# Sixteen rows of a gather fetched by SyncE with addresses from registers, and GpSimd's gather cut to 112 partitions

## What is computed

```python
msg = relu(x[src] + edge_attr)                       # layer 0
h = 2 * x + segment_sum(msg, dst)
f = gelu(bn(h) @ W1.T + b1) @ W2.T + b2
x = layernorm(x + bn(h + f))
h = gelu((x[src] + edge_attr) @ W1m + b1m)           # layer 1
agg = segment_sum(h @ W2m + b2m, dst) / max(degree, 1)
u = gelu(agg @ W1u + b1u) @ W2u + b2u
out = layernorm(x + layernorm(x + u) * gamma + beta) # in outline
```

## Time and profile before

| | |
|---|---|
| three runs | 2637.56, 2638.18, 2649.71 us; median 2638.18 us |
| the profiled execution | span 2139.9 us from its first to its last instruction; its own time on the device is not given beside it |
| granted TensorE clock, mean | 0.975 |
| instructions | 38235 |
| POOL | busy 1593.0 us, 74% |
| PE, DVE, ACT | busy 87%, 71%, 60% |
| DMA | 569.42 MB, mean 266 GB/s |

### The profile page before, as it was taken

One profiled execution on the slowest core, in us unless ns is written; L12 is line 12 of the kernel. 1 busy time (PEld: TensorE's weight loads), 2 busy tenths in 40 slices (PEclk: granted clock), 3 DMA queues, 4 the chain that ended last, 5 costly groups with the idle time before them and its releaser, 6 DMA issues.

```text
span 2139.9 us, 38235 instructions
## 1 busy us (share of the span) xinstructions
PE 1853.7 (87%) x9034; PEld 1516.1 (71%) x9034; DVE 1515.9 (71%) x3743; ACT 1287.3 (60%) x2642; POOL 1593.0 (74%) x1695
## 2 busy tenths in 40 slices
PE   4998888888888888888879899899899899999997
PEld 3876767666666666666667777777777777777775
DVE  4676666666666666666666787877777887787786
ACT  5766566566566565565555565656665665665664
POOL 7777777777777777777577777777777777777774
PEclk9999999999999999999999999999999999999998
DMA  8999999999999999999788787777778777777783
GB/s 251 341 336 310 320 309 318 306 311 312 316 303 315 314 306 318 306 314 316 234 268 241 216 232 224 232 227 227 229 227 234 225 227 224 227 235 223 226 236 107
DMA packets 349112, 569.42 MB, mean 266 GB/s; under 512 B 48328, under 2 KB 214212, under 8 KB 349044
## 3 DMA queue, kind: packets, MB, share of 16 engines
q1 hardware_dynamic: 268858, 349.78, 51.3%
q0 software_dynamic: 79824, 218.08, 33.3%
q10 hardware_dynamic: 362, 0.85, 0.1%
HBM read 500.59 MB, written 67.94 MB: 266 GB/s over the span
## 4 chain that ended last, share of the span: by engine, by line
POOL 47%; issue 18%; PE 15%; DMA 13%; DVE 5%; DVEq 1%; ACT 1%; ACTq 0%; POOLq 0%
POOL m_all L678 46%; DMA m_all<-in_x,src_p 7%; DMA m_all<-y_scratch,src_u 5%; PE bank L1136 4%; PE bank L1202 3%; PE bank L1161 2%; PE bank L1244 1%; PE bank L1107 1%; DVE bank L1549 1%; DVEq L1482 1%; DVE m_all L1526 1%; PE bank L1044 1%; DMA win_i<-in_dst 1%; ACT m_all L854 1%; PE bank L1118 1%
## 5 line engine op out<-in xcount | busy, mean ns | idle before, releaser
L678 POOL DMA_INDIRECT m_all<-y_scratch,src_u x831 | 789.3, 950 | 256.0 <-issue 238.9
L678 POOL DMA_INDIRECT m_all<-in_x,src_p x816 | 777.3, 953 | 248.8 <-issue 233.7
L1136 PE MATMUL bank<-m_all,sel 128*128 128x257 f32 x1664 | 454.2, 396 | 141.2 <-ACT m_all L854 139.7
L1202 PE MATMUL bank<-w1m_sb,e_all 128*128 128x256 f32 x2040 | 514.2, 393 | 1.5 <-DVE m_all L1669 1.5
L854 ACT ACTIVATE m_all<-m_all 128x512 f32<-128x512 f32 x415 | 261.1, 629 | 379.3 <-DVE m_all L1526 378.3
L1136 PEld LDWEIGHTS bank<-m_all,sel 128*128 128x128 f32 x1664 | 299.7, 192 | 244.3 <-issue 126.6
L1526 DVE TENSOR_TENSOR m_all<-bank,m_all 128x512 f32<-128x512 f32 x415 | 285.1, 688 | 235.8 <-DMA m_all<-in_x,src_p 215.8
L906 ACT ACTIVATE m_hi<-bank 128x512 fp32r<-128x512 f32 x412 | 245.7, 596 | 295.2 <-DVE bank L1549 293.2
L1549 DVE TENSOR_TENSOR bank<-bank,m_all 128x512 f32<-128x512 f32 x415 | 288.9, 696 | 183.6 <-DMA m_all<-y_scratch,src_u 122.9
L1202 PEld LDWEIGHTS bank<-w1m_sb,e_all 128*128 128x128 f32 x2040 | 380.6, 197 | 45.2 <-DVE m_all L1669 2.0
L1244 PE MATMUL bank<-m_lo,sel 128*128 128x256 f32 x824 | 263.7, 344 | 86.3 <-DVE sel L1446 74.5
(11 more groups left out here) (196 smaller groups left out, 1948.5 us busy)
## 6 DMA issues: line engine op xcount, KB each, us to landing
e_all<-in_edge SPq DMA_DIRECT2D x416, 256.0 KB, 5.5
e_all<-in_edgeT SPq DMA_DIRECT2D x204, 256.0 KB, 3.7
ez<-in_edgeT SPq DMA_DIRECT2D x103, 384.0 KB, 5.0
z_scratch<-zc SPq DMA_DIRECT2D x103, 384.0 KB, 6.0
e_all<-z_scratch SPq DMA_DIRECT2D x103, 256.0 KB
m_all<-y_scratch,src_u POOLq DMA_INDIRECT x831, 3.7
e_all<-z_scratch SPq DMA_DIRECT2D x103, 128.0 KB
m_all<-in_x,src_p POOLq DMA_INDIRECT x816, 5.6
```

What stands on the lines that cost most here:

```text
L678: pool.indirect_dma_start(out=m_sb[n % ROUND][:, t, :], out_offset=None, in_=table, in_offset=bass.IndirectOffsetOnAxis(ap=sources(g, u), ...
L1136: return pe.matmul(psum[:, 0:D + 1], selection[:, u, :].bitcast(F32), m_all[:, slot, u % 2, 0:D + 1], start=(u == 0), stop=(u == TILES - 1 ...
L1202: last = pe.matmul(z_bank(s)[:, t * D:(t + 1) * D], eT_sb[s % ERING][:, k, t * P:(t + 1) * P], w1m_sb[:, k, :], start=(k == 0), stop=(k == ...
```

## The change

SP fetches the last 16 rows (partitions 112 to 127) of the last tile of every second group, g = 3, 5, ..., 101, in both passes, one row of 1 KB per transfer. The row's number comes from a new list `row_src`, read four numbers at a time into SP's registers. POOL's gather of these tiles names 112 partitions. DVE waits for SP's rows (`row_in`) beside POOL's gather. DVE also makes the list, with two small copies at the start. The sixteen rows of pair p = 4g + 3 = 8b + 15 are issued in four batches of four, at SP's steps 8b + 4, 8b + 6, 8b + 8 and 8b + 10.

```diff
+SHARED = 16
+AT_ONCE = 4
...
+        row_src = sb("row_src", [G, 2, SHARED], I32)
...
+        def shared(g):
+            return g % 2 == 1 and 2 <= g < G - 1
+
+        def rows_in(i, s):
+            q, j = divmod(s, PAIRS)
+            if j < 3 or q % 2 == 0 or known(i) and not shared(PER_ROUND * i + q):
+                return None
+            return 16 * SHARED * (i + q // 2)
...
+            def gather_rows(table, second, n):
+                b, r = divmod(n // 2 - 2, SHARED // AT_ONCE)
+                g = 2 * b + 3
+                if n % 2 or b < 0 or not shared(g):
+                    return
+                slot = (PAIRS * g + 3) % ROUND
+                if not r and second:
+                    if b == 0:
+                        sp.wait_ge(y_out, 16 * C)
+                        sp.wait_ge(xab_out, 32 * C)
+                        sp.wait_ge(a_clear, C)
+                    if PAIRS * g + 3 >= ROUND:
+                        sp.wait_ge(added, M + PAIRS * g + 3 - ROUND + 1)
+                elif not r:
+                    if b == 0:
+                        sp.wait_ge(row_src_made, 1)
+                    if PAIRS * g + 3 >= ROUND:
+                        sp.wait_ge(pair_summed, PAIRS * g + 3 - ROUND + 1)
+                numbers = nc.values_load_multi_w_load_instructions(
+                    row_src[g:g + 1, second, r * AT_ONCE:(r + 1) * AT_ONCE], engines=[sp.engine], min_val=0, max_val=N - 1,
+                    skip_runtime_bounds_check_because="they number nodes")[1]
+                for k, v in enumerate(numbers):
+                    p = P - SHARED + r * AT_ONCE + k
+                    sp.dma_start(m_all[p:p + 1, slot, 1, 0:D], table[bass.ds(v, 1), :]).then_inc(row_in[slot // TILES], 16)
...
             def edges_first(n, early=False):
...
+                gather_rows(x, 0, n)
 
             def edges_second(n, early=False):
...
+                gather_rows(y_dram, 1, n)
...
                 for t in range(first, 2):
                     u = 2 * j + t
+                    rows = P - SHARED if u == TILES - 1 and shared(g) else P
                     pool.indirect_dma_start(
-                        out=m_sb[n % ROUND][:, t, :], out_offset=None, in_=table,
-                        in_offset=bass.IndirectOffsetOnAxis(ap=sources(g, u), axis=0),
+                        out=m_sb[n % ROUND][0:rows, t, :], out_offset=None, in_=table,
+                        in_offset=bass.IndirectOffsetOnAxis(ap=sources(g, u)[0:rows, :], axis=0),
...
+                if i == 1:
+
+                    dve.tensor_copy(row_src[:, 0, :], ends_f[1].rearrange("g (p u) -> g p u", u=TILES)[:, P - SHARED:P, TILES - 1])
+                    dve.tensor_copy(row_src[:, 1, :], ends_f[1][:, GROUP - SHARED:GROUP]).then_inc(row_src_made, 1)
...
                 dve.wait_ge(m_in[s], m_used(i))
+                if rows_in(i, s) is not None:
+                    dve.wait_ge(row_in[s // TILES], rows_in(i, s))
...
                 dve.wait_ge(m_in[s], m_used_again(i) - 16 * tile_of(i, s) - (16 if s == ROUND - 1 else 0))
+                if rows_in(i, s) is not None:
+                    dve.wait_ge(row_in[s // TILES], rows_in(i, s) + rows_first_pass)
```

More of the change, by code:

```diff
@@ L360, in build @@
         ends_ready, lists_turned, lists_made = map(sem, ("ends_ready", "lists_turned", "lists_made"))
+        row_src_made, row_in = sem("row_src_made"), sems("row_in", 2)
         bn_made, acc_zero, w_fused, w_kept = map(sem, ("bn_made", "acc_zero", "w_fused", "w_kept"))
@@ L463, in e_used_again @@
             return each * (2 * i) + each * (s // ERING + 1) + 16 * (M // ERING)
+        def shared(g):
[5 more added lines that the diff above has]
+            return 16 * SHARED * (i + q // 2)
+        rows_first_pass = 16 * SHARED * (ROUNDS - 1)
+        assert not shared(1) and shared(3) and G % 4 == 0 and not shared(G - 1) and shared(G - 3)
         def last_pair(i, s):
```

## The result

The changed kernel takes 2892.1 us (median of four runs, 2888.7 to 2899.8) against 2638.5 us of the kernel before (2637.6 to 2649.7): ratio 1.0957 [1.0931, 1.0984], slower by 254 us. Predicted were 2633 us, in a range of 2622 to 2675.

A forecast was written before the change was run, and what follows sets the result against it. The prediction took POOL's full queue of gathers to bound both passes. Its only non-zero term, 5.9 us saved by shorter gathers, gave 2638.2 - 5.9 = 2632.3, rounded to 2633 us, range 2622 to 2675.

The forecast's parts named there:

- What bounds the kernel: POOL's full gather queue sets both passes, 1.25 us per gather, 20.0 us per two groups; 498.3 us outside the span carried over.
- What it adds to SP: SP's queue: 16 transfers and four reads per two groups, 7.2 + 1.6 us, making 14.5 of 20.0 us; costed at nothing.
- the forecast's 2 to 12 us saved: Whole kernel: shorter POOL gathers save 2 to 12 us, time 2626 to 2640 us; chance 0.41.
- rival 1: POOL's 112-row gather takes as long as one of 128; sum 0 to +1.1 us, 2639 us; chance 0.24.
- rival 3: SP becomes the bound from 0.79 us per row; at 1.0 us 330 us more, near 2960; chance 0.13.
- POOL's part: 100 gathers of 112 rows for 128, each 59 ns shorter (between 0 and 118), saving 5.9 us.
- The DMA engines: One-row transfers sit whole on one engine, raising its pass 1 share from 0.94 to 0.98 to 1.04; costed at nothing.
- rival 2: One DMA engine fills up in pass 1; at 130 ns per row +40 us, 2673 us; chance 0.17.
- Waits and late rows: SP's slot wait is met on arrival and rows land 5 us before DVE uses them; costed at nothing.
- rival 4: Rows land late for DVE, beyond 5 us of margin; costs only if it grows, then the same end as rival 2 or rival 3.
- DVE's instructions and the two small copies: DVE's 100 waits with arithmetic, nothing (uncovered 7 us); two copies at the start, nothing, at most 1.1 us.

The follow-up runs named there:

- e0_before: The kernel before, unchanged, run again to get a second trace at the slow pace: 2637.2 us, 0.9999 of before.
- z2: Changed kernel with fixed row numbers, register reads, moves and arithmetic replaced by plain counts on a spare semaphore, at the slow pace: 2821.7 us, 1.0708 of before.
- e1_gather112: Kernel before with POOL's part only: 98 gathers name 112 partitions, SP fetches nothing; slow pace: 2633.8 us, 0.9981 of before.
- e2: Changed kernel with its 1600 one-row transfers from fixed row numbers, no register reads or address arithmetic; slow pace: 2648.0 us, 1.0035 of before.
- e7: Kernel before plus, at 400 places on SP, a loop of four turns counting a spare semaphore, no row transfers; quick pace: 2149.9 us, 1.0006 of before.
- sessions 2 and 3: Two sets of runs, each made together on one chip, at the quick pace; the kernel before took 2149.0 and 2150.0 us.
- session 6: A set of runs made together on one chip, at the slow pace: the change and two of its part variants; the kernel before took 2635.6 us.
- e6: Changed kernel with one read of one number and one computed address per batch of four, other three rows fixed; quick pace: 2148.9 us, 1.0003 of before.

## Why the prediction was wrong

**What bounds the kernel.** This failed first. "The 498.3 us between them are outside every view; the edit puts nothing there that I can see, and I carry them over whole" took the second pace for work before and after the trace. e0_before shows the span to be 2640.6 us when the run is 2642. Everything built on the POOL clock (1.25 us per gather, 20.0 us for two groups, SP's 14.5 of 20.0) was true of the trace and not of the executions that were timed. At the slow pace the clock of pass 1 is 1196.0 / 816 x 16 = 23.5 us for two groups. POOL now waits for others, at the start of each group, the two waits below:

```profile
1005.05 0.95 POOL L678 DMA_INDIRECT m_all<-in_x,src_p  x1 [2.01 <-remote]
1006.30 0.95 POOL L678 DMA_INDIRECT m_all<-in_x,src_p  x1 [0.30 <-issue]
...
1016.75 0.95 POOL L678 DMA_INDIRECT m_all<-in_x,src_p  x1 [1.97 <-PE bank L1136]
```

**What it adds to SP.** The step that carries the loss: "It has room, narrowly at the dear end... I cost it at nothing". The sum of it was right at the quick pace: arithmetic 37 ns, move 29, transfer 253 (240 in pass 2), reads 495 ns, so 9.4 us for four batches where 8.8 were worked out, and nothing at the end (0.9992, an interval of -4 to 0 us, which can't tell the forecast's 2 to 12 us saved from rival 1's nothing). The room was smaller than forecast all the same: in pass 1 SP had 116 us of longer gaps left in 1028.6, 2.3 us of 20.0 where 5.5 were worked out. At the slow pace the four batches are 18.5 us. Less the four reads at their median of 0.5 us, a row costs (4.63 - 0.5) / 4 = 1.03 us. This is rival 3's place and mechanism: its threshold was 0.79 us per row, and at 1.0 it gave 330 us. With the true clock of 23.5 us in pass 1 the same line gives 18.5 + 5.7 - 23.5 = 0.7 us, only 35 us for its 50 times, and nothing in pass 2, whose clock is 25.1 us. The rest comes from what SP does besides: in pass 1 it has 308 us of other instructions and 141 us of gaps beside them, 449 us or 8.8 us per two groups for the 5.7 assumed, and 18.4 (940 us) + 8.8 = 27.2 of the 27.8 us that two groups take after. So SP's records account for the new length of pass 1. The other instructions did not grow as a sum (306 us in e0_before, at the same pace). The edge loads did, from 328 to 419 ns in the middle, but they read 418 ns at the quick pace too, so that is no mark of the slow one. What rival 3 had wrong was its reason: "none has an address from a register". The register address is 66 ns more (37 + 29), and plain counts in its place keep 76% of the loss (z2). What the loss follows is how many small instructions SP executes beside its transfers, and no term of the sum priced a pause per instruction.

**POOL's part.** Mis-sized: 59 ns were taken, and the 100 gathers of 112 rows read 932 ns in the middle against 949 for the others, 934 against 956 in the mean, at the quick pace and nearly the same at the slow one. The third of these rows, POOL at the quick pace, is the shared tile of group 49:

```profile
507.16 0.95 POOL L726 DMA_INDIRECT m_all<-in_x,src_p  x1 [0.30 <-issue]
508.41 0.95 POOL L726 DMA_INDIRECT m_all<-in_x,src_p  x1 [0.30 <-issue]
509.67 0.93 POOL L726 DMA_INDIRECT m_all<-in_x,src_p  x1 [0.30 <-issue]
```

That is 17 to 22 ns, 1.7 to 2.2 us for 100, nearer to rival 1's nothing than to the 5.9 us of the sum. e1_gather112 alone gave -4 us [-9, -1] at the slow pace, where POOL isn't the bound, of which the shorter gathers would explain some 2; the rest is open. What the Trainium skill says (DMA: Bandwidth & Descriptors, "Anatomy of one DMA — SWDGE (gpsimd) path"), that many descriptors can be emitted before their number costs noticeably, agrees with these rows.

**The DMA engines (rival 2).** Right, costed at nothing. A one-row transfer left two packets (272058 on SP's queue for 268858 before, 3200 for 1600 transfers), which fits data that go whole through one engine, as the prediction had read from ACT's packets. In pass 1 the share rose from 0.94 to 0.96 at 313 GB/s for 312 and the time stood still at the quick pace; at the slow pace e2 has all the transfers for 10 us, where the rival put 40.

**Waits and late rows (rival 4).** Right at the quick pace: DVE waited for the rows twice, 6.2 us in all. At the slow pace it waited 39 times and 233 us; the rows are late because SP is, so it is rival 3's end, as the prediction had it. DVE's instructions and the two small copies show no cost at the quick pace.

**What stays open.** What makes the slow pace. Single instructions of POOL and DVE last as long in both (the gathers 949 ns in the middle, DVE's adds of line 1605 or 1549 695 and 696 ns in the mean), while SP's instructions stall. PE's matmuls are a little longer (line 1136: 425 ns in the mean for 396), at a granted clock of 0.888 in e0_before for 0.975 in the trace of before. The clock alone isn't the reason: one run of e7 at the quick pace had a granted clock of 0.845 and took 2160.8 us. It isn't a matter of one chip: by their records sessions 2 and 3 (quick) and session 6 (slow) ran on the chip with the same number. Nor was it settled why counts alone cost 46 us in one session and 100 us in another.

One rival for the stalls was not tested: the recording of the execution itself. The traces of the slow pace have all instructions (43529 of the change in both), but few of the records of semaphores: 14492 in e0_before for 54487 in before, 17159 for 57453 for the change. So records were lost at the slow pace and hardly or not at the quick one, and no run was made with less recorded. What made one may have made the other, or the recording may hold up an engine whose instructions come dense. It also means that "another core or an unknown queue" and "remote" in the slow views are partly missing records, and that who released a wait there is less sure than at the quick pace.

## What to carry to other kernels

Set the span of the trace against the time of the runs before anything else: when they differ by more than a few us, the trace may be of another pace, and its bound may not be the bound that is timed. When work is moved to a queue that seems free, count its instructions and not only their durations, and price them also at a slower issue (0.3 to 0.4 us each here), above all where one instruction becomes many small ones. And compare parts within one session: the same kernel lay 46 us above before in one and 100 us in another.

## What the runs showed of the hardware

In these runs the same program took 2149 or 2638 us, with all kernels of a session at one pace. At the slow one SyncE stalled some 0.7 us again and again, more than once in five instructions in the change (1542 of 6803), and the stalls hit counts, register moves, branches and transfers alike. A loop of four turns did not help against straight instructions (4.08 and 3.91 us per 13), with 62 and 90 instruction packets. A gather of 112 rows takes GpSimd 932 ns and one of 128 rows 949: most of the time belongs to the instruction and not to its rows. At the quick pace a one-row transfer with its address from a register issues in 0.24 to 0.25 us, with 0.07 us of arithmetic and move before it, and a read of four numbers into registers takes 0.50 us, of one number 0.46 us (e6).
